# Preparation of a graph layer's weights: a weight loaded and split in quarters, two splits and the turning of x moved, 8 warm-up products for 14

## The reference

```python
z_l = jnp.einsum('bnd,ed->bne', h, W_lang)
z_g = jnp.einsum('bnd,ed->bne', h, W_grav)
v = jnp.einsum('bnd,ed->bne', h, W_V)
zn = z_l / jnp.maximum(jnp.linalg.norm(z_l, axis=-1, keepdims=True), EPS)
A_l = jnp.maximum(jnp.einsum('bnd,bmd->bnm', zn, zn), 0.0) * not_eye
d2 = jnp.maximum(sq + jnp.swapaxes(sq, -1, -2) - 2.0 * jnp.einsum('bnd,bmd->bnm', z_g, z_g), 0.0)
A_g = jnp.exp(-d2 / (2.0 * sigma * sigma)) * not_eye
K = w_l * K_l + (1.0 - w_l) * K_g      # K_l, K_g: A_l, A_g masked by adj, rows divided by their sums
out = jnp.einsum('bnm,bmd->bnd', K, v)
out = jnp.einsum('bnd,ed->bne', out, W_O)
# and the result is _layernorm(x + out)
```

## Time and profile before

| | us |
|---|---|
| median of 3 runs | 706.07 (705.94 to 707.54) |
| the profiled execution | 705.9 |
| its span | 704.1 |
| TensorE matmul busy | 679.8 (97%) |
| DVE busy | 515.9 (73%) |
| ACT busy | 366.3 (52%) |
| POOL busy | 135.0 (19%) |

### The profile page before, as it was taken

The page is one execution under the profiler, slowest core; times in us unless marked ns, Lnnn a source line. Parts: engine busy times, 40 slices in busy tenths (PEclk is TensorE's granted clock), DMA queues, the critical chain, the costliest instruction groups (busy, mean ns, idle before and its releaser), DMA issues.

```text
span 704.1 us, 10990 instructions
## 1 busy us (share of the span) xinstructions
PE 679.8 (97%) x3026; PEld 561.9 (80%) x3026; DVE 515.9 (73%) x1382; ACT 366.3 (52%) x707; POOL 135.0 (19%) x284
## 2 busy tenths in 40 slices
PE   8899999999999999999999999999999999999971
PEld 7788888888888888888888888888888888888751
DVE  4554868788788868788697878778787878778571
ACT  4434445645466554645456564546555564545545
POOL 3302021111222121112222022122222111122212
PEclk9999999999999999999999999999999999999997
DMA  9221736373665547374664557364554647262322
GB/s 293 54 58 36 218 98 187 120 207 108 198 177 157 172 156 201 104 206 122 194 177 145 169 164 205 108 191 137 186 170 146 184 149 199 80 196 94 106 89 90
DMA packets 141446, 106.50 MB, mean 151 GB/s; under 512 B 40048, under 2 KB 115568, under 8 KB 141424
## 3 DMA queue, kind: packets, MB, share of 16 engines
q1 hardware_dynamic: 140864, 104.66, 49.6%
q0 software_dynamic: 288, 1.05, 0.4%
q10 hardware_dynamic: 272, 0.52, 0.2%
HBM read 65.80 MB, written 40.40 MB: 151 GB/s over the span
## 4 chain that ended last, share of the span: by engine, by line
PE 92%; ACT 3%; DVE 2%; DMA 1%; issue 1%; POOL 1%; ACTq 0%; POOLq 0%; DVEq 0%
PE bank L1041 90%; PE bank L1063 2%; ACT y L638 1%; DMA xs<-in_L_gnn_W_lang 1%; ACT junk_a L630 1%; DMA out_y<-y 0%; DVE y L938 0%; POOL rstd L493 0%; DVE p_lo L732 0%; ACT xs L588 0%; DVE work L905 0%; DVE v_lo L791 0%; ACT kt_hi L621 0%; DVE hT_lo L755 0%; DVE hT_raw L718 0%
## 5 line engine op out<-in xcount | busy, mean ns | idle before, releaser
L1041 PE MATMUL bank<-hT_lo,m_hi 128*128 128x512 f32 x512 | 168.0, 389 | 0.0
L577 ACT CAST p_hi<-bank 128x512 fp32r<-128x512 f32 x128 | 73.6, 588 | 107.0 <-PE bank L1041 107.0
L1041 PE MATMUL bank<-hT_hi,m_lo 128*128 128x512 f32 x320 | 124.5, 389 | 0.0
L791 DVE TENSOR_TENSOR p_lo<-bank,p_hi 128x512 fp32r<-128x512 f32 x128 | 85.3, 687 | 41.1 <-ACT p_hi L577 39.4
L1041 PEld LDWEIGHTS bank<-hT_lo,m_hi 128*128 128x128 f32 x512 | 96.1, 188 | 19.9
L577 ACT CAST v_hi<-bank 128x512 fp32r<-128x512 f32 x64 | 34.7, 590 | 135.3 <-PE bank L1041 135.3
L1041 PE MATMUL bank<-wvo_hi,hT_hi 128*128 128x512 f32 x256 | 99.9, 390 | 0.0
L1041 PE MATMUL bank<-wvo_lo,hT_hi 128*128 128x512 f32 x256 | 99.6, 389 | 0.0
L1041 PE MATMUL bank<-wvo_hi,hT_lo 128*128 128x512 f32 x256 | 99.6, 389 | 0.0
L1041 PE MATMUL bank<-p_hi,hT_hi 128*128 128x512 f32 x256 | 99.6, 389 | 0.0
L1041 PE MATMUL bank<-p_lo,hT_hi 128*128 128x512 f32 x256 | 99.6, 389 | 0.0
(11 more groups left out here) (111 smaller groups left out, 1200.4 us busy)
## 6 DMA issues: line engine op xcount, KB each, us to landing
x_blk<-in_x SPq DMA_DIRECT2D x128, 128.0 KB, 3.0
x_nat<-in_x SPq DMA_DIRECT2D x32, 512.0 KB, 4.5
out_y<-y SPq DMA_DIRECT2D x32, 512.0 KB, 3.0
x_spill<-xs SPq DMA_DIRECT2D x30, 512.0 KB, 3.4
xq<-x_spill SPq DMA_DIRECT2D x120, 128.0 KB, 2.9
k_spill<-work SPq DMA_DIRECT2D x30, 256.0 KB, 2.2
work<-k_spill SPq DMA_DIRECT2D x120, 64.0 KB, 2.1
r_row<-r_spill SPq DMA_DIRECT2D x32, 128.0 KB, 3.4
```

The source lines that it names most:

```text
L577: nc.scalar.copy(dst, src).then_inc(proj_hi, 1)
L791: nc.vector.tensor_tensor(dst, src, hi.bitcast(F32), ALU.subtract).then_inc(proj_ready, 1)
L1041: last = pe.matmul(dst, lhsT, rhs, start=(n == 0), stop=(n == len(steps) - 1))
```

## The change

W_lang is loaded in four quarters, 0 and 2 by SP, 1 and 3 by ACT, each with a semaphore of its own, and the splitting of quarter k waits for its quarter. POOL waits for all four. Two of the four splits of W_grav (k = 0, 1) are put ahead of unit 0 on ACT and DVE; the other two follow units 0 and 1, where before one followed each of units 0 to 3. DVE turns graph 0 of pair 0 after unit 14 (G3) instead of unit 7 (G1), and makes its low part after unit 16 (WVO 0) instead of unit 10 (G2); graph 1 is turned after unit 17 instead of 16, and split after unit 18 as before. `WARM` is 8.

```diff
-        w_loaded = [[sem(f"w_loaded{i}{h}") for h in range(2)] for i in range(3)]
+        w_loaded = [[sem(f"w_loaded{i}{h}") for h in range((DT, 2, 2)[i])] for i in range(3)]
...
-        TURN_AT = {prep_units.index((UPPER, G, 1)): 0, prep_units.index((WVO, None, 0)): 1}
-        SPLIT_AT = {prep_units.index((UPPER, G, 2)): 0, prep_units.index((WVO, None, 1)): 1}
+        TURN_AT = {prep_units.index((UPPER, G, DT - 1)): 0, prep_units.index((MIRROR, G, 2)): 1}
+        SPLIT_AT = {prep_units.index((WVO, None, 0)): 0, prep_units.index((WVO, None, 1)): 1}
...
-        WARM = 14
+        WARM = 8
...
+        def load_quarter(queue, k):
+
+            queue.dma_start(raw[L][:, k], w_lang[k * P:(k + 1) * P, :]).then_inc(w_loaded[L][k], 16)
+
+        def part_loaded(i, k):
+
+            return w_loaded[i][k if i == L else k // 2]
...
-            load_w(sp, L, w_lang, 0)
+            for k in (0, 2):
+                load_quarter(sp, k)
...
-            for h in range(2):
-                pool.wait_ge(w_loaded[L][h], 16)
+            for k in range(DT):
+                pool.wait_ge(w_loaded[L][k], 16)
...
-            load_w(act, L, w_lang, 1)
+            for k in (1, 3):
+                load_quarter(act, k)
...
-                act.wait_ge(w_loaded[i][k // 2], 16)
+                act.wait_ge(part_loaded(i, k), 16)
...
+            for k in range(2):
+                weight_hi(G, k)
...
-                if kind == UPPER and g == L:
-                    weight_hi(G, i)
+                if kind == UPPER and g == L and i < 2:
+                    weight_hi(G, 2 + i)
...
+            for k in range(2):
+                weight_lo(G, k)
...
-                if kind == UPPER and g == L:
-                    weight_lo(G, i)
+                if kind == UPPER and g == L and i < 2:
+                    weight_lo(G, 2 + i)
```

## The result

| | before | changed kernel |
|---|---|---|
| median | 706.01 us (705.92 to 707.54, 4 runs) | 701.76 us (701.41 to 702.16, 4 runs) |
| profiled execution's span | 704.13 us | 700.32 us |
| ratio | | 0.9935, 95% interval 0.9918 to 0.9952 |

What follows compares the result with a forecast made beforehand. TensorE's dense products, 620 of 704 us, were taken as the bound, so only an earlier start helps. The sum was 706.07 - 1.4 - 0.4 - 2.7 = 701.6 us, own range 700.9 to 702.6, 8 in 10 range 699.8 to 703.7.

Steps and rivals of the forecast that it cites:

- The bound: From 34.53 us only matmuls bound the kernel; time saved in the preparation is handed through to the end.
- The total: All parts together gain 4.5 us: 1.4, 0.4 and 2.7, giving 701.6 us.
- Part 1: W_lang in quarters: first block's products start at 5.7 and end at 8.4 us, gain 1.4 us (1.0 to 1.8).
- The price of the added issue: One more DMA issue on SP and ACT, 0.45 us each; no landing shifts by more than that.
- Part 2: Eight warm-up products end at 5.0 us, before TensorE's first work; removal free, loss taken as 0 (ends 0 and 1.4).
- late clock: Rival, 20 in 100: 1.2 GHz kept until about 8.9 us in the first block, 1.4 us lost, 703.0 us.
- Part 3: Two W_grav splits ahead of the first block: the halt before G0's last products goes, gain 0.4 us.
- Part 4: Turn of pair 0's x behind the last block: holes before WVO close, WVO starts at 23.7 us, gain 2.7 us.
- The cover ahead of pair 0: x's second low part ends at 33.9 us, TensorE needs it at 35.3: 1.4 us; further delay paid one for one.
- The tail: Near the kernel's end: the forecast kept the fall to 1.2 GHz behind TensorE's idle of 3.3 us.
- The price of the rival: Tail clock rival, 11 in 100: no fall to 1.2 GHz behind the tail's idle, 1.6 us saved, 700.0 us.

Runs made afterwards that it cites:

- the halves: Changed kernel with W_lang loaded in two halves again, 8 warm-up products kept: median 704.63 us.
- the later turn: Changed kernel with x of pair 0 turned and split one WVO block later still: median 704.45 us.
- second trace of before: Kernel before, unchanged, profiled once more: median 707.05 us, profiled execution 708.1 us.
- the filled tail: Changed kernel with 12 products of unused result put into TensorE's idle of 3.2 us in the tail: median 700.19 us, ratio to before 0.991.
- turn as before: Changed kernel with x of pair 0 turned and split where the kernel before did it, after G1 and G2: median 706.24 us.

## Why the prediction was right

**The bound.** That the rest of the kernel hands an earlier start through was right to 0.2 us: pair 0 to the end took 664.3 and 664.4 us.

**The total** came out closer than the working. The sum was 4.5 us; the traces give 3.97 at pair 0. That the medians differ by 4.25, and the forecast is missed by 0.2 only, is in part luck: four executions each, of kernels whose executions differ by more than that.

**Part 1** was put at 1.4 us, from 1.0 to 1.8; it measured 1.03 in the traces (1.15 against the halves). The first quarter landed at 4.09 us (4.2 forecast) and the first product came at 5.59 (5.7). The step that failed is the one that named the limit. I had the second quarter at 5.0 us and the block's end set by quarters and splits; the second quarter, ACT's first, landed 0.2 us behind the first, at 4.3 (4.2 to 4.4 in all nine traces with quarters). DVE's timeline shows the four splits without a pause:

```profile
4.76 2.53 DVE L745 TENSOR_TENSOR p_lo<-xs,p_hi 128x512 fp32r<-128x512 f32 x4 [4.76 <-ACT p_hi L545]
```

The last was done at 7.3, not 7.6, and TensorE never waited for one. What set the end of the block was the clock: the first product was followed after 0.57 us, the second after 0.35, all later ones after 0.23. The term was mis-sized by 0.4 us, and the block's end at 8.4, which I forecast, is reached when the clock is up at 5.7 (8.44 with the later turn).

The price of the added issue was too low. I had it shift no landing by more than 0.45 us. In the changed kernel's trace the halves of W_grav landed at 8.3 and 9.5 us instead of 7.3 and 8.6, and the second half of W_O at 15.2 instead of 11.4. TensorE needs it for the first W_O turn at 16.56, so 1.3 us of cover were left. The quarters go with it: in the five traces with halves W_O's second half landed at 11.4 to 11.8 us, in the nine with quarters at 11.3 to 15.2, in six of them after 13. Why it differs among the nine is open. ACT's first split of W_grav began at 8.29 (7.4 forecast) and held up its copy of L0's result to 9.33, off TensorE's path:

```profile
8.29 1.14 ACT L545 CAST p_hi<-work 128x512 fp32r<-128x512 f32 x2 [1.80 <-DMA work<-in_L_gnn_W_grav]
9.33 0.58 ACT L555 CAST m_hi<-bank 128x512 fp32r<-128x512 f32 x1
```

**Part 2.** The rival "late clock" was right in kind and too dear: 1.4 us was worked out for a rise at 8.9, the traces show rises up to 7.45, which put L1 0.85 us behind the best one. (Three slips of the working, none of them in the sum: the block's end for that rise is 9.9 when redone, not 9.8; the rise before, which I worked out as 5.6 from the spacing, stands at 5.36 in the trace's record; the turn and the low part of x last 1.24 and 1.22 us in the earlier trace rows, not 1.16 and 1.13.) I had tied it to the number of products; ten products with no hole did not bring it forward. Of the rule of the Trainium skill that I weighed ("TensorE: Matmul & The Clock Gate", section "What's actually happening"), the part on variation from run to run is what these traces agree with: 4.84 to 7.45 us. They go beyond the 500 ns to either side that the section gives, and the measurement decides: 2.35 us lie between the rises behind the same eight products. Fewer warm-ups pay because they are out of the way, 0.7 us between eight and fourteen.

**Part 3** was put at 0.4 us and came out as 0.44 in the two traces, but the working was right by luck: I took the late split as given, without its cause. The moved splits are sufficient (8.10 to 8.12 us in all eight traces that have them), not needed in every execution: without them the section took 8.12, 8.54, 8.69 or 8.95 us. What they avoid is a meeting of DVE and POOL, which I had left unexplained in the row of 17.12; the section is up to 0.85 us longer with it. In these traces the one that begins second pays. In the second trace of before that was DVE, by 0.05 us:

```profile
14.74 1.30 POOL L445 TENSOR_TENSOR v_lo<-xq,v_hi 128x512 fp32r<-128x512 f32 x1
14.79 1.79 DVE L732 TENSOR_TENSOR p_lo<-work,p_hi 128x512 fp32r<-128x512 f32 x1
```

With the W_grav splits at their old places in the changed kernel it was POOL, by 0.06 us, and TensorE lost nothing. This is read from the traces; no run took POOL's steps away. The page "SBUF — State Buffer" of the Trainium skill, section "SBUF: two separate sides", says that a VectorE instruction with two SBUF inputs and a GpSimd one that reads SBUF exclude each other for a whole instruction; the two steps that stretched side by side, 1.37 for 0.68 us and 1.62 for 1.29, agree in kind.

**Part 4** was put at 2.7 us and measured 2.5 (9.85 to 7.36), alone as well as in company. I had WVO waiting for the last W_O split at 23.7; it started at 24.27, 0.4 of the difference from the late clock. The wait is there, and the rest is its length: the row of 24.24 above has WVO's weight load waiting 0.22 us for DVE's last W_O split. DVE's last two:

```profile
22.85 1.28 DVE L768 TENSOR_TENSOR hT_lo<-bank,hT_hi 128x512 fp32r<-128x512 f32 x2
```

They were done at 24.13, and WVO began 0.15 us later, as it does in all fourteen traces. From the last transpose to WVO took 0.36 us where I gave 0.1. The cover ahead of pair 0 was 1.2 us, for 1.4 forecast: the second low part ended at 34.65 us and TensorE came at 35.88. It ran out with the turn one WVO block later.

```profile
33.43 1.22 DVE L739 TENSOR_TENSOR hT_lo<-hT_raw,hT_hi 128x1024 fp32r<-128x1024 f32 x1
```

**What the sum left out** is the clock behind the holes. In five traces with the turn at its old place the clock fell behind them in four and cost 1.5 to 1.6 us; in the nine with it moved it never did. Over the untraced executions the share is smaller: about one in three for the kernel before, by the averaged clock, five of twelve with its tail filled, and seven of nine for the changed kernel with its tail filled and the turn at its old place. The first measurement of before had three executions near 706.0 and one at 707.54, so its 4.25 us may understate what the change brings on average: against the 53 executions of before beside the experiments (median 706.63) it is 4.9 us. That is an estimate, since the changed kernel was not run beside them. The prediction came from a trace without the fall, and its closeness owes something to that.

**The tail** kept its fall in the changed kernel's trace, as forecast, and lost it in single executions of two variants (the spans of 698.8 and 700.6 us). With the later turn it was twice as long. The price of the rival, 1.6 us, is what the filled tail gave.

## What to carry to other kernels

Ahead of a dense stretch of TensorE, sum the lengths of its own steps and move everything that other engines do for later consumers behind the last step that TensorE waits for; check the cover of what is moved against its first consumer. Price a hole at its length and again at what the clock may lose behind it: here holes of 1.9 us in all cost 2.5 us in each execution and 1.6 us more in some, from about a third of them in one kernel to seven of nine in another. Read TensorE's weight loads as well as its products: two waits of 0.2 us that the rows of the products don't show stand there. Where the time of the unchanged kernel has more than one level, a second trace of it is worth more than another edit; the granted clock, averaged over each execution, then says how many of the untraced ones are of either kind.

## What was not expected of the hardware

- The clock fell to 1.2 GHz behind a stretch in which TensorE was busy for 2.12 of 3.40 us, with no single hole over 1 us (turn as before); in the first trace of before the same holes brought no fall.
- The clock's first rise lay anywhere from 5.10 to 7.45 us from the span's start behind the same eight products.
- Twelve products without a use, 2.9 us of them in an idle of 3.2 us, made the kernel 1.6 us faster.
- A DVE split and a POOL step that overlap stretched by 0.3 to 1.1 us. The one that began second stretched more: DVE's split from 0.68 to 1.79 us where POOL began 0.05 us ahead (second trace of before), POOL's step from 1.29 to 1.77 where DVE began 0.06 us ahead.
- With one load of the first weight on each queue split in two, and the same bytes in all, the second half of W_O landed at 11.3 to 15.2 us instead of 11.4 to 11.8.
